# Local attention layers: the mask moved from TensorE to VectorE, the subtraction of the row maximum from VectorE to GpSimd, and the inverse norms computed by logarithm, exponential and a Newton step

## Chip, cores and metric

The kernel runs on one core of one Trainium2 chip. The time is the device time of one execution in microseconds. The kernel before has a median of 3261.2 us over three runs (3251.27, 3261.2 and 3266.76 us).

## What is computed

An input of 2048 tokens with 128 features goes through one global attention layer with 16 heads and a relation bias, and then through six local layers (`DEPTH` = 6). The change touches the local layers alone. Cut to that part, with 16 heads of 64 features and windows of 32 tokens, each local layer is:

```python
def l2norm(t):
    return t / jnp.maximum(jnp.linalg.norm(t, axis=-1, keepdims=True), 1e-12)

qkv = x @ Wqkv                                   # x is the shifted input
q = l2norm(q) * qs;  k = l2norm(k) * ksc
q = q * cos * scale + rotate_half(q) * sin * scale
k = k * cos * inv + rotate_half(k) * sin * inv
...
sim = jnp.einsum('bhwie,bhwje->bhwij', bq, bk2) * QK_SCALE      # 8.0
sim = jnp.where(mask, -jnp.finfo(sim.dtype).max, sim)
attn = jax.nn.softmax(sim, -1)
out = jnp.einsum('bhwij,bhwje->bhwie', attn, bv2)
x = out @ Wo + x
x = (a * gelu(gate)) @ W2 + b2 + x               # a, gate from layernorm(shift(x)) @ W1 + b1
```

The softmax runs over 64 keys: the window of the query and the one before it.

## The kernel before

The tokens are cut into `NB` = 16 blocks of 128. A local layer handles its blocks one after the other, so there are `NT` = 96 blocks in all. `local_layers` writes out one program per engine by hand, over the same list of `STEPS` (-1 to 101). In step `s` an engine works on several blocks at once, at different stages: projections for block `s`, transposes of q and k for `s-1`, scores, softmax and product with v for `s-2`, the output projection for `s-4`, the feed-forward part for `s-5` and `s-6`. Each engine executes its queue in the order of the program, and semaphores (`m[...]`) tie the engines together.

Names that matter below:

- TensorE in one step: scores S (L1255 mask, L1259), projection Q (L1235), transposes of k (L1242, from `kn`), projection K, output projection (L1284), transpose of `xn` (L1292), projection V, transposes of q, transpose of `xa` (L1308), W2 (L1314), transposes of the probabilities `pr`, transposes of `ot`, W1 (L1333), product with v (L1345).
- Its results lie in three PSUM buffers `R`, used in rotation in the order of `RING`. A use waits until the use three turns earlier has been read (`read_by`): Q waits for `g_done` of the feed-forward product in the step before, K waits for the reader of S, V waits for `sqq_done`.
- VectorE: maximum (L1513), subtraction (L1517), rotary products of q and k (L1504 to L1506), sums of squares (L1538, L1562), sum of the softmax (L1555), `bn_stats` (L1578), `ot` (L1589), `gT` (L1598), `xn` (L1607), in about this order.
- GpSimd: `kn` (L1446), root for q (L1435 maximum with 1e-24, L1437 power), scaling of `pr` by the inverse norms of q (L1455), the two rotary additions (L1460, L1462), `xmb` (L1468), `tab` (L1481), root for k (L1435, L1437), then `var` and `rstd` (L1489, L1493) of the layer norm.
- ScalarE: copies of kT (L1364, L1369), square of q (L1376), exponential (L1381), square of k (L1386), copy of v (L1391), copies of qT, prT and otT (L1352), Gelu (L1418), copies of xsT (L1425 to L1428). The table of the exponential and that of Gelu are loaded once each in a step.

The inverse norm of q isn't applied to q but to the scores: the kernel takes the maximum over unscaled scores, subtracts it, and multiplies the difference by the inverse norm. The mask is 0 or -1e25 and is written into PSUM as the first of two accumulated products.

Of the kernel before, what the change touches and what calls it, by code (L numbers as in the profile page):

```python
# [17 lines left out]
ALU = mybir.AluOpType  # L18
# [1039 lines left out]
def local_layers(nc, io):  # L1058
    with ExitStack() as ctx:
# [14 lines left out]
        mask = sb("mask", [P, 2, 2 * WIN], BF16)  # L1074
        ident = sb("ident2", [P, P])
        identb = sb("identb", [P, P], BF16)
# [9 lines left out]
        rnq = sb("rnq", [P, 2, LH])  # L1086
        rnk = sb("rnk", [P, LH])
# [33 lines left out]
            ssqq_done ssqk_done clampq_done clampk_done rnq_done rnk_done q_added k_added kn_done qT_done kT_done qT_ready  # L1121
            kT_ready s_done mx_done sub_done scaled_done exp_done sum_done rden_done pT_done pT_ready pv2_done o_ready
# [45 lines left out]
        with nc.Block() as block:  # L1168
            @block.sync
            def _(sp):  # L1170
                for dst, src in ((xm[:, 1:NB + 1, :], io["x1"].rearrange("(b p) d -> p b d", p=P)),
                                 (rope[:], io["rope"]), (mask32[:], io["mask"]), (ident[:], io["ident"])):
                    sp.dma_start(dst, src).then_inc(m["init_dma"], 16)
                load(sp, 0)

            @block.gpsimd
            def _(pool):
                n = 0
                for tile, value in ((half1[:], -0.5), (vs[:], 0.0), (v2[:], 0.0), (kT[:], 0.0), (zeros[:], 0.0), (xsT[:], 0.0)):
                    pool.memset(tile, value).then_inc(m["init_pool"], 1)  # L1180
                    n += 1

                pool.wait_ge(m["init_dve"], 2)
                pool.wait_ge(m["init_pool"], n)
                pool.tensor_scalar(mv16[:, :, 1], mv16[:, :, 1], 1e-5, None, ALU.add).then_inc(m["init_pool"], 1)
                pool.wait_ge(m["init_pool"], n + 1)
                pool.tensor_tensor(rs16[:], mv16[:, :, 1], half1[:, 0:NB], ALU.pow).then_inc(m["init_pool"], 1)

            @block.vector
            def _(dve):  # L1190
                dve.wait_ge(m["init_dma"], 16 * 4)
# [8 lines left out]
                dve.tensor_copy(identb[:], ident[:])  # L1200
                dve.tensor_copy(mask[:], mask32[:])
# [14 lines left out]
        read_by = {"S": "sub_done", "Q": "sqq_done", "kT": "kT_ready", "K": "sqk_done", "V": "v_ready", "qT": "qT_ready",  # L1216
# [6 lines left out]
        with nc.Block() as block:  # L1223
            @block.tensor
            def _(pe):
# [19 lines left out]
                for s in STEPS:  # L1245
                    n = s - 2
                    if has(n):
# [102 lines left out]
            def _(act):  # L1350
# [3 lines left out]
                for s in STEPS:  # L1354
# [52 lines left out]
                    if has(n):  # L1407
# [3 lines left out]
                        copy(otT[:].rearrange("p a b -> p (a b)"), flat[slot["oT", n]], "oT_ready")  # L1411
                    n = s - 5
# [18 lines left out]
            def _(pool):  # L1431
                def root(i, n, dst, summed, clamped, done):

                    pool.wait_ge(m[summed], n + 1)
                    pool.tensor_scalar(ssq[:, i, :], ssq[:, i, :], 1e-24, None, ALU.max).then_inc(m[clamped], 1)  # L1435
                    pool.wait_ge(m[clamped], n + 1)
                    pool.tensor_tensor(dst, ssq[:, i, :], half1[:], ALU.pow).then_inc(m[done], 1)  # L1437

                for s in STEPS:
                    n = s - 1  # L1440
                    if has(n):
                        pool.wait_ge(m["k_added"], n + 1)
                        pool.wait_ge(m["rnk_done"], n + 1)
                        if n > 0:
                            pool.wait_ge(m["kT_done"], n)
                        pool.tensor_tensor(kn[:].rearrange("p (h d) -> p h d", d=LD), k1[:].rearrange("p (h d) -> p h d", d=LD),  # L1446
                                           rnk[:].unsqueeze(2).broadcast_to([P, LH, LD]), ALU.mult).then_inc(m["kn_done"], 1)
                    if has(n):
                        root(0, n, rnq[:, n % 2, :], "ssqq_done", "clampq_done", "rnq_done")
                    n = s - 2  # L1450
                    if has(n):
                        pool.wait_ge(m["sub_done"], n + 1)
                        pool.wait_ge(m["rnq_done"], n + 1)
                        p = pr[:, n % 2].rearrange("p i a k -> p (i a) k")
                        pool.tensor_tensor(p, p, rnq[:, n % 2, :].unsqueeze(2).broadcast_to([P, LH, 2 * WIN]), ALU.mult)\  # L1455
                            .then_inc(m["scaled_done"], 1)
# [27 lines left out]
                    if has(n):  # L1484
                        root(1, n, rnk[:], "ssqk_done", "clampk_done", "rnk_done")
# [10 lines left out]
            def _(dve):  # L1496
# [11 lines left out]
                for s in STEPS:  # L1508
                    n = s - 2
                    if has(n):  # L1510
                        dve.wait_ge(m["s_done"], n + 1)
                        scores = flat[slot["S", n]].rearrange("p (h k) -> p h k", k=2 * WIN)
                        dve.tensor_reduce(mx[:], scores, AX.X, ALU.max).then_inc(m["mx_done"], 1)  # L1513
                        dve.wait_ge(m["mx_done"], n + 1)
                        if n > 1:
                            dve.wait_ge(m["pT_done"], n - 1)
                        dve.tensor_tensor(pr[:, n % 2].rearrange("p i a k -> p (i a) k"), scores,  # L1517
                                          mx[:].unsqueeze(2).broadcast_to([P, LH, 2 * WIN]), ALU.subtract)\
                           .then_inc(m["sub_done"], 1)
# [14 lines left out]
                    if has(n):  # L1534
                        dve.wait_ge(m["sqq_done"], n + 1)
                        if n > 0:
                            dve.wait_ge(m["rnq_done"], n)
# [20 lines left out]
                    if has(n):  # L1558
                        dve.wait_ge(m["sqk_done"], n + 1)
                        if n > 0:  # L1560
                            dve.wait_ge(m["rnk_done"], n)
# [169 lines left out]
```

## Time and profile before

| | |
|---|---|
| median of three runs | 3261.2 us |
| the profiled execution's own time | 3259.23 us |
| its span | 3257.4 us |
| global attention ends, first projection of the local layers | about 1500 us |
| TensorE busy | 2989.6 us (92%) |
| VectorE busy | 2433.3 us (75%) |
| GpSimd busy | 2283.7 us (70%) |
| ScalarE busy | 2033.3 us (62%) |

The span is the time between the first and the last instruction of the profile; 1.8 us of the execution lie around it. In the part after 1600 us GpSimd is busy for 375 of 400 us and TensorE for 394 of 400 us. A busy time of TensorE includes pipelining and isn't its best rate. In a timeline row the first number is the start in us from the span's start, the second the duration; "x4" says how many instructions were merged, and brackets show how long the engine was idle before it, and who released it. PEld is the loading of weights, which overlaps the products.

### The profile page before, as it was taken

How to read it: one execution, taken by the hardware profiler on the slowest of the kernel's cores; microseconds unless marked ns; L12 is line 12 of the kernel's file. 1: busy time of each engine (PE TensorE's matmuls, PEld its weight loads, DVE VectorE, ACT ScalarE, POOL GpSimd, SP SyncE). 2: the span in 40 equal slices, each digit the busy share in tenths (PEclk: the TensorE clock that was granted, in tenths of full speed). 3: DMA queues.
4: the chain of work that ended last, by engine and by line, in shares of the span. 5: the costliest groups of instructions: out<-in, count | busy, mean ns of one | idle time of the engine just before them, and what ended most of it. 6: DMA issues, size and time to landing. Idle time of an engine off the chain costs nothing.

```text
span 3257.4 us, 122555 instructions
## 1 busy us (share of the span) xinstructions
PE 2989.6 (92%) x53463; PEld 2278.3 (70%) x53463; DVE 2433.3 (75%) x3495; ACT 2033.3 (62%) x2669; POOL 2283.7 (70%) x1528
## 2 busy tenths in 40 slices
PE   4389999999999999994999999999999999999998
PEld 2267777777777777772677777777777777777776
DVE  4777777777777777734878778787877878787775
ACT  2345555555555555552677777777777777777775
POOL 1635555555555454306999999999999999999995
PEclk8589999999999999997999999999999999999999
DMA  5544445444444444404322233223223322322221
GB/s 116 101 80 86 77 84 88 85 79 86 81 83 84 78 84 84 84 5 124 82 64 63 69 79 83 59 68 96 66 67 81 83 58 69 94 68 67 68 76 45
DMA packets 253990, 251.90 MB, mean 77 GB/s; under 512 B 81999, under 2 KB 198624, under 8 KB 253328
## 3 DMA queue, kind: packets, MB, share of 16 engines
q1 hardware_dynamic: 251776, 243.67, 35.4%
q8 instruction: 423, 6.93, 1.0%
q14 instruction: 111, 0.91, 0.1%
q10 hardware_dynamic: 1680, 0.40, 0.1%
HBM read 96.22 MB, written 40.37 MB: 42 GB/s over the span
## 4 chain that ended last, share of the span: by engine, by line
PE 38%; ACT 8%; issue 4%; DVE 1%; POOL 1%; SPq 0%; DMA 0%; ACTq 0%; DVEq 0%; POOLq 0%
PE R L1235 11%; PE R L1242 10%; PE R L1345 5%; PE R L1259 5%; PE R L1333 4%; ACT kT L1364 3%; ACT sq L1376 3%; ACT kT L1369 2%; PE psB L1314 2%; PE R L1255 1%; PE psA L1308 0%; DVE mx L1513 0%; DVE ssq L1538 0%; DVE k L1504 0%; DMA xs_f<-xm 0%
## 5 line engine op out<-in xcount | busy, mean ns | idle before, releaser
L660 ACT ACTIVATE prob<-psS 128x1024 f32<-128x1024 f32 x512 | 524.0, 1024 | 598.7 <-PE psS L537 591.2
L824 DVE TENSOR_TENSOR colmax<-psS,colmax 128x1024 f32<-128x1024 f32 x480 | 587.3, 1224 | 309.1 <-PE psS L537 307.9
L537 PE MATMUL psS<-diag,pst 128*128 128x64 bf16 x16384 | 585.9, 195 | 26.6 <-issue 26.4
L1235 PE MATMUL R<-wqkv,xsT 128*128 128x512 f32 x1152 | 573.2, 620 | 37.1 <-ACT sq L1376 31.3
L537 PEld LDWEIGHTS psS<-diag,pst 128*128 128x128 f16 x16384 | 519.1, 99 | 87.3 <-issue 33.9
L529 PE MATMUL psS<-qst,kst 48*128 48x128 bf16 (+1 forms) x8192 | 382.0, 221 | 125.6 <-DMA pst<-p_parts 89.9
L758 POOL TENSOR_TENSOR rel<-rel,rec 128x1024 f32<-128x1024 f32 x64 | 151.7, 2370 | 484.7 <-DVE rec L837 484.7
L1364 ACT ACTIVATE kT<-R 64x1024 f32<-64x1024 f32 x192 | 195.7, 1019 | 423.7 <-PE R L1242 422.6
L529 PEld LDWEIGHTS psS<-qst,kst 48*128 48x128 bf16 (+1 forms) x8192 | 236.1, 95 | 282.4 <-issue 173.0
L1235 PEld LDWEIGHTS R<-wqkv,xsT 128*128 128x128 f32 x1152 | 196.9, 190 | 227.4 <-issue 159.6
L571 PE MATMUL psO<-prob,v 128*9 128x128 f32 x8192 | 326.6, 275 | 12.6 <-issue 11.3
L1437 POOL TENSOR_TENSOR rnq<-ssq,half 128x16 f32<-128x16 f32 x96 | 281.7, 2934 | 8.0
L1437 POOL TENSOR_TENSOR rnk<-ssq,half 128x16 f32<-128x16 f32 x96 | 281.2, 2930 | 8.0
L1589 DVE TENSOR_TENSOR ot<-R,rden 128x1024 f32<-128x1024 f32 x96 | 117.6, 1225 | 208.8 <-PE R L1345 208.7
L837 DVE RECIPROCAL rec<-tot 128x128 f32<-128x128 f32 x256 | 238.7, 939 | 0.0
L1460 POOL TENSOR_TENSOR q<-q 128x1024 f32<-128x1024 f32 x96 | 227.0, 2364 | 6.8 <-DVE q L1506 6.8
L1462 POOL TENSOR_TENSOR k<-k 128x1024 f32<-128x1024 f32 x96 | 227.8, 2372 | 0.3 <-DVE k L1506 0.3
L1284 PEld LDWEIGHTS psA<-wo,otT 128*128 128x128 f32 x1536 | 186.3, 192 | 44.4 <-issue 44.4
L571 PEld LDWEIGHTS psO<-prob,v 128*9 128x9 f32 x8192 | 174.0, 90 | 43.7 <-issue 15.1
L1259 PEld LDWEIGHTS R<-kT,qT 128*32 128x32 f32 x6144 | 162.0, 110 | 40.8 <-issue 40.7
L1345 PE MATMUL R<-v,prT 128*32 128x128 f32 x6144 | 187.6, 274 | 2.8 <-ACT prT L1352 2.8
L1259 PE MATMUL R<-kT,qT 128*32 128x128 f32 x6144 | 187.8, 274 | 0.0
(190 smaller groups left out, 6076.2 us busy)
## 6 DMA issues: line engine op xcount, KB each, us to landing
v<-vs SPq DMA_DIRECT2D x576, 128.0 KB, 2.4
pst<-p_parts SPq DMA_DIRECT2D x512, 128.0 KB, 4.9
p_parts<-stage SPq DMA_DIRECT2D x64, 512.0 KB, 3.0
v<-vs SPq DMA_DIRECT2D x384, 64.0 KB, 2.0
wqkv<-in_L_ffn_Wqkv SPq DMA_DIRECT2D x18, 512.0 KB
q_stack<-qpart SPq DMA_DIRECT2D x6, 512.0 KB
qst<-q_stack SPq DMA_DIRECT2D x32, 96.0 KB, 5.4
wo<-in_L_ffn_Wo SPq DMA_DIRECT2D x6, 512.0 KB
```

Source lines behind the costliest of these rows:

```text
L529: pe.matmul(dst[:, hp, P * p:P * (p + 1)], kst[r, pair, P * jb:P * (jb + 1)], qst[r, par, pair, :], start=(p == 0), stop=False, skip_group ...
L537: last = pe.matmul(o, pst[:, par, g, P * jb:P * (jb + 1)], diag[:, par, g, h0:h0 + HH // 2, :], start=False, stop=(g == NG - 1), skip_grou ...
L571: last = pe.matmul(psO[32 * c:32 * c + HD + 1, P * s:P * (s + 1)], v9[:, jb, HH * half + hl, :], prob[:, jb % 2, col:col + P], start=(jb = ...
L660: act.activation(prob[:, st % 2, :], psS[:, slot_of("b", st)].rearrange("p a b -> p (a b)"), ACT.Exp)\
L824: dve.tensor_tensor(dst, src, dst, ALU.max).then_inc(a_read, 1)
L837: dve.reciprocal(rec[:, r, cols], tot[:, r, cols]).then_inc(rr_done, 1)
L1235: last = pe.matmul(R[slot[kind, n]][:, c, :], xsT[:, n % 3, :], w[:, INNER * which + 512 * c:INNER * which + 512 * (c + 1)], start=True, s ...
L1242: last = pe.transpose(o[:, P * i:P * (i + 1)], src[:, P * i:P * (i + 1)], ident[:])
L1259: last = pe.matmul(o[WIN * w:WIN * (w + 1), P * i:P * (i + 1)], qT[:, par, i, WIN * w:WIN * (w + 1)], kT[:, par, i, :, WIN * w:WIN * (w + 2)],
L1345: last = pe.matmul(o[WIN * w:WIN * (w + 1), P * i:P * (i + 1)], prT[:, i, WIN * w:WIN * (w + 1)], v2[:, par, w, :, i, :], start=True, stop ...
L1364: act.activation(kT[r, par, :, hp, WIN:WIN + P], keys[r], ACT.Copy)
L1437: pool.tensor_tensor(dst, ssq[:, i, :], half1[:], ALU.pow).then_inc(m[done], 1)
```

## The change

- TensorE no longer multiplies the mask in. The scores start their own PSUM groups.
- VectorE adds the mask from `mask32` while it moves the scores from PSUM into `pr` (new semaphore `masked_done`), and then takes the maximum from `pr`. The PSUM buffer of S is free after the addition.
- GpSimd subtracts the maximum from `pr` in place, after `mx_done`, and then scales `pr` as before.
- The two powers on GpSimd (L1437) go. One maximum with 1e-24 over both sums of squares (128x32) stands in their place; ScalarE takes the logarithm and the exponential of -0.5 times it (128x32 each), placed after the copy of otT and ahead of Gelu; GpSimd then makes a Newton step of four instructions on 128x32. Everything that waited for `rnq_done` or `rnk_done` waits for `rn_done`. The power for `rstd` (L1493) stays.
- ScalarE loads the set `natural_log_exp_and_others` by an instruction of its own ahead of the softmax's exponential, behind the wait for `scaled_done`.
- Two small copies at the start of the local layers go.

```diff
-                        mk = mask[:, 0 if n % NB == 0 else 1, :]
-                        for half in range(2):
-                            pe.matmul(R[slot["S", n]][:, half, :], identb[:], mk.unsqueeze(1).broadcast_to([P, PAIRS, 2 * WIN]),
-                                      start=True, stop=False, skip_group_check=True)
                         for i in range(PAIRS):
                             for w in range(NW):
                                 last = pe.matmul(o[WIN * w:WIN * (w + 1), P * i:P * (i + 1)], qT[:, par, i, WIN * w:WIN * (w + 1)],
                                                  kT[:, par, i, :, WIN * w:WIN * (w + 2)],
-                                                 start=False, stop=True, skip_group_check=True)
+                                                 start=True, stop=True, skip_group_check=True)
...
                         act.wait_ge(m["scaled_done"], n + 1)
+                        act.preload_act_table_set("natural_log_exp_and_others")
...
+                    n = s
+                    if has(n):
+                        act.wait_ge(m["clamp_done"], n + 1)
+                        act.activation(logs[:], ssq[:].rearrange("p a h -> p (a h)"), ACT.Ln).then_inc(m["log_done"], 1)
+                        act.wait_ge(m["log_done"], n + 1)
+                        if n > 1:
+                            act.wait_ge(m["scaled_done"], n - 1)
+                        act.activation(rn[:, n % 2].rearrange("p a h -> p (a h)"), logs[:], ACT.Exp, scale=-0.5)\
+                           .then_inc(m["root_done"], 1)
...
-                    if has(n):
-                        root(0, n, rnq[:, n % 2, :], "ssqq_done", "clampq_done", "rnq_done")
                     n = s - 2
                     if has(n):
+                        pool.wait_ge(m["mx_done"], n + 1)
+                        p = pr[:, n % 2].rearrange("p i a k -> p (i a) k")
+                        pool.tensor_tensor(p, p, mx[:].unsqueeze(2).broadcast_to([P, LH, 2 * WIN]), ALU.subtract)\
+                            .then_inc(m["sub_done"], 1)
                         pool.wait_ge(m["sub_done"], n + 1)
-                        pool.wait_ge(m["rnq_done"], n + 1)
...
-                        root(1, n, rnk[:], "ssqk_done", "clampk_done", "rnk_done")
+                        x, y, t = ssq[:].rearrange("p a h -> p (a h)"), rn[:, n % 2].rearrange("p a h -> p (a h)"), newton[:]
+                        pool.wait_ge(m["ssqk_done"], n + 1)
+                        pool.tensor_scalar(x, x, 1e-24, None, ALU.max).then_inc(m["clamp_done"], 1)
+                        pool.wait_ge(m["root_done"], n + 1)
+                        pool.tensor_tensor(t, y, y, ALU.mult).then_inc(m["newton_done"], 1)
+                        pool.wait_ge(m["newton_done"], 3 * n + 1)
+                        pool.tensor_tensor(t, t, x, ALU.mult).then_inc(m["newton_done"], 1)
+                        pool.wait_ge(m["newton_done"], 3 * n + 2)
+                        pool.tensor_scalar(t, t, -0.5, 1.5, ALU.mult, ALU.add).then_inc(m["newton_done"], 1)
+                        pool.wait_ge(m["newton_done"], 3 * n + 3)
+                        pool.tensor_tensor(y, y, t, ALU.mult).then_inc(m["rn_done"], 1)
...
-                        dve.tensor_reduce(mx[:], scores, AX.X, ALU.max).then_inc(m["mx_done"], 1)
-                        dve.wait_ge(m["mx_done"], n + 1)
                         if n > 1:
                             dve.wait_ge(m["pT_done"], n - 1)
-                        dve.tensor_tensor(pr[:, n % 2].rearrange("p i a k -> p (i a) k"), scores,
-                                          mx[:].unsqueeze(2).broadcast_to([P, LH, 2 * WIN]), ALU.subtract)\
-                           .then_inc(m["sub_done"], 1)
+                        p = pr[:, n % 2].rearrange("p i a k -> p (i a) k")
+                        allowed = mask32[:, 0 if n % NB == 0 else 1, :].unsqueeze(1).broadcast_to([P, LH, 2 * WIN])
+                        dve.tensor_tensor(p, scores, allowed, ALU.add).then_inc(m["masked_done"], 1)
+                        dve.wait_ge(m["masked_done"], n + 1)
+                        if n > 0:
+                            dve.wait_ge(m["sub_done"], n)
+                        dve.tensor_reduce(mx[:], p, AX.X, ALU.max).then_inc(m["mx_done"], 1)
```

## Rows read from the trace of the kernel before

**Rows 1.** Waits, 1600 to 3200 us: total, times, longest.
```profile
PE R L1235 <- ACT sq L1376: 24.3, 87, 0.3
```
**Rows 2.** Chain that ended last: start, us, what; the mask's products.
```profile
2828.31 0.54 PE R L1255 x2
```
**Rows 3.** Timeline of one step of the ring, all engines: start, duration.
```profile
2812.97 1.22 DVE L1513 TENSOR_REDUCE mx<-R 128x16 f32<-128x1024 f32 x1 [0.16 <-PE R L1259]
...
2814.23 1.22 DVE L1517 TENSOR_TENSOR pr<-R,mx 128x1024 f32<-128x1024 f32 x1
...
2816.06 1.90 POOL L1455 TENSOR_TENSOR pr<-pr,rnq 128x1024 f32<-128x1024 f32 x1
...
2817.92 2.37 POOL L1460 TENSOR_TENSOR q<-q 128x1024 f32<-128x1024 f32 x1
...
2821.05 0.14 PEld L1242 LDWEIGHTS R<-ident,q 128*128 128x128 f32 x1 [0.24 <-issue]
...
2822.36 0.27 PE L1308 MATMUL psA<-ident,xa 128*128 128x128 f32 x1
...
2823.15 1.21 DVE L1562 TENSOR_REDUCE ssq<-sq 128x16 f32<-128x1024 f32 x1
...
2824.01 1.04 PE L1242 MATMUL R<-ident,ot 128*128 128x128 f32 x8
...
2824.44 0.25 POOL L1435 TENSOR_SCALAR ssq<-ssq 128x16 f32<-128x16 f32 x1 [0.73 <-DVE ssq L1562]
...
2825.50 1.05 ACT L1352 ACTIVATE otT<-R 128x1024 f32<-128x1024 f32 x1
...
2828.38 1.22 DVE L1589 TENSOR_TENSOR ot<-R,rden 128x1024 f32<-128x1024 f32 x1 [2.07 <-PE R L1345]
...
2829.52 0.85 DVE L1598 SCALAR_TENSOR_TENSOR gT<-R,b_cols,gl 128x128 f32<-128x128 f32 x3
...
2830.30 0.34 DVE L1607 TENSOR_SCALAR xn<-xs_f,mv,rstd 128x128 f32<-128x128 f32 x1
...
2830.66 0.30 PEld L1235 LDWEIGHTS R<-wqkv,xsT 128*128 128x128 f32 x2 [0.20 <-issue]
...
2830.80 1.23 DVE L1513 TENSOR_REDUCE mx<-R 128x16 f32<-128x1024 f32 x1 [0.16 <-PE R L1259]
```
**Rows 4.** Groups by line, 1600 to 3257 us: busy, mean ns; idle before.
```profile
L1468 POOL TENSOR_TENSOR xmb<-xm,b_rows 128x128 f32<-128x128 f32 x96 | 44.4, 463 | 2.3 <-DVE xa L1574 2.3
...
L1428 ACT ACTIVATE xsT<-psA 64x1 f32<-64x1 f32 x83 | 12.8, 154 | 0.0
```
**Rows 5.** Timeline of an early step, in which TensorE waits for GpSimd.
```profile
1518.32 1.90 POOL L1446 TENSOR_TENSOR kn<-k,rnk 128x1024 f32<-128x1024 f32 x1
...
1520.27 0.86 PEld L1242 LDWEIGHTS R<-ident,kn 128*128 128x128 f32 x8 [3.05 <-POOL kn L1446]
...
1521.20 1.88 PE L1235 MATMUL R<-wqkv,xsT 128*128 128x512 f32 x4
```
**Rows 6.** Timelines of GpSimd, then VectorE, in a step with late `kn`.
```profile
2240.06 0.23 POOL L1489 TENSOR_SCALAR var<-mv 128x1 f32<-128x1 f32 x1 [0.85 <-DVE mv L1582]
...
2240.92 1.90 POOL L1446 TENSOR_TENSOR kn<-k,rnk 128x1024 f32<-128x1024 f32 x1
```
```profile
2241.81 1.09 DVE L1607 TENSOR_SCALAR xn<-xs_f,mv,rstd 128x128 f32<-128x128 f32 x1
2242.83 1.21 DVE L1513 TENSOR_REDUCE mx<-R 128x16 f32<-128x1024 f32 x1
```
**Rows 7.** Line 1607 in all steps: duration in ns, minimum/median/maximum.
```profile
L1607 DVE TENSOR_SCALAR xn<-xs_f,mv,rstd x96: 333/346/1658, 1581.2 to 3247.0; 128x128 f32<-128x128 f32 x96
```
**Rows 8.** Timeline of the drain, after the last projections.
```profile
3208.40 1.90 POOL L1455 TENSOR_TENSOR pr<-pr,rnq 128x1024 f32<-128x1024 f32 x1
...
3209.22 1.28 ACT L1381 ACT_TABLE_LOAD   x1
```

More of the change, by code:

```diff
@@ L1073, in local_layers @@
         mask32 = sb("mask32", [P, 2, 2 * WIN])
-        mask = sb("mask", [P, 2, 2 * WIN], BF16)
         ident = sb("ident2", [P, P])
-        identb = sb("identb", [P, P], BF16)
         xsT = sb("xsT", [P, 3, P])
@@ L1085, in local_layers @@
         ssq = sb("ssq", [P, 2, LH])
-        rnq = sb("rnq", [P, 2, LH])
-        rnk = sb("rnk", [P, LH])
+        rn = sb("rn", [P, 2, 2, LH])
+        newton = sb("newton", [P, 2 * LH])
+        logs = sb("logs", [P, 2 * LH])
         kn = sb("kn", [P, INNER])
@@ L1120, in local_layers @@
         names = """init_dma init_dve init_pool w_dma xT_done xT_ready q_done k_done v_done sqq_done sqk_done tq_done tk_done
-            ssqq_done ssqk_done clampq_done clampk_done rnq_done rnk_done q_added k_added kn_done qT_done kT_done qT_ready
-            kT_ready s_done mx_done sub_done scaled_done exp_done sum_done rden_done pT_done pT_ready pv2_done o_ready
+            ssqq_done ssqk_done clamp_done log_done root_done newton_done rn_done q_added k_added kn_done qT_done kT_done qT_ready
+            kT_ready s_done masked_done mx_done sub_done scaled_done exp_done sum_done rden_done pT_done pT_ready pv2_done o_ready
             oT_done oT_ready wo_done x2_done st_done lnv_done eps_done rstd_done xn_done xnT_done xnT_ready h_done
@@ L1199, in _ @@
                 dve.memset(xm[:, 0, :], 0.0)
-                dve.tensor_copy(identb[:], ident[:])
-                dve.tensor_copy(mask[:], mask32[:])
                 dve.wait_ge(m["init_pool"], 8)
@@ L1215, in local_layers @@
         earlier = {t: turns[i - 3] for i, t in enumerate(turns) if i >= 3}
-        read_by = {"S": "sub_done", "Q": "sqq_done", "kT": "kT_ready", "K": "sqk_done", "V": "v_ready", "qT": "qT_ready",
+        read_by = {"S": "masked_done", "Q": "sqq_done", "kT": "kT_ready", "K": "sqk_done", "V": "v_ready", "qT": "qT_ready",
                    "pT": "pT_ready", "oT": "oT_ready", "h": "g_done", "O": "o_ready"}
@@ L1431, in _ @@
             def _(pool):
[L1432 to L1437, printed above, removed]
                 for s in STEPS:
@@ L1442, in _ @@
                         pool.wait_ge(m["k_added"], n + 1)
-                        pool.wait_ge(m["rnk_done"], n + 1)
+                        pool.wait_ge(m["rn_done"], n + 1)
                         if n > 0:
@@ L1446, in _ @@
                         pool.tensor_tensor(kn[:].rearrange("p (h d) -> p h d", d=LD), k1[:].rearrange("p (h d) -> p h d", d=LD),
[L1447 to L1449 removed]
+                                           rn[:, n % 2, 1, :].unsqueeze(2).broadcast_to([P, LH, LD]), ALU.mult).then_inc(m["kn_done"], 1)
                     n = s - 2
                     if has(n):
+                        pool.wait_ge(m["mx_done"], n + 1)
+                        p = pr[:, n % 2].rearrange("p i a k -> p (i a) k")
+                        pool.tensor_tensor(p, p, mx[:].unsqueeze(2).broadcast_to([P, LH, 2 * WIN]), ALU.subtract)\
+                            .then_inc(m["sub_done"], 1)
                         pool.wait_ge(m["sub_done"], n + 1)
[L1453 to L1455 removed]
+                        pool.wait_ge(m["rn_done"], n + 1)
+                        pool.tensor_tensor(p, p, rn[:, n % 2, 0, :].unsqueeze(2).broadcast_to([P, LH, 2 * WIN]), ALU.mult)\
                             .then_inc(m["scaled_done"], 1)
@@ L1536, in _ @@
                         if n > 0:
-                            dve.wait_ge(m["rnq_done"], n)
+                            dve.wait_ge(m["rn_done"], n)
                         dve.tensor_reduce(ssq[:, 0, :], sq[:].rearrange("p (h d) -> p h d", d=LD), AX.X, ALU.add)\
@@ L1560, in _ @@
                         if n > 0:
-                            dve.wait_ge(m["rnk_done"], n)
+                            dve.wait_ge(m["rn_done"], n)
                         dve.tensor_reduce(ssq[:, 1, :], sq[:].rearrange("p (h d) -> p h d", d=LD), AX.X, ALU.add)\
```

## The prediction

> **What bounds the kernel now.** I read the groups by line first. They show GpSimd with two powers of 2.93 us in each step, which looks like the engine to relieve. The waits say otherwise: in the local layers TensorE waits for ScalarE's square of q, 87 times for 0.3 us at most [rows 1], and for next to nothing else. The chain that ended last is accordingly almost all TensorE, with one passage through ScalarE's copies of kT and the square, and the mask's products lie on it with 0.54 us a step [rows 2]. The timeline of one step then gives the order on each engine. From one start of the maximum on VectorE to the next it takes 2830.80 - 2812.97 = 17.83 us [rows 3]. Below, all times are us after that start (0), before the change:
>
> maximum 0, subtraction 1.26, GpSimd's scaling 3.09, its q addition 4.95, TensorE's first load of weights for the q transposes 8.08, transpose of xa 9.39, end of the ot transposes 12.08, ScalarE's copy otT 12.53, VectorE's ot 15.41, gT 16.55, xn 17.33, load for projection Q 17.69, maximum again 17.83 [rows 3].
>
> Two things are to be seen there. First, the q addition ends at 7.32, and TensorE wants it at 8.08: GpSimd has only 0.76 us in hand. Second, VectorE runs ot, gT and xn back to back after the product with v, and is done at 17.67, 0.16 us before it starts the maximum. Projection Q waits, by the ring of PSUM buffers, for gT, which ends at 17.40, and Q's load is at 17.69. So the stretch after the product with v is nearly as long on VectorE (ot, gT, xn) as on TensorE (mask, scores).
>
> **Part by part.**
>
> *The mask's products.* 0.54 us a step leave TensorE, 96 times, 52 us if nothing else were late [rows 2]. But VectorE is late next. From ot to the next maximum it needs 1.14 + 0.78 + 0.27 = 2.19 us (xn lasts 0.34 and the next instruction starts 0.07 before its end) against the 2.42 us it has now. Without the mask, the scores would be done 0.54 earlier and VectorE 0.23 earlier. So this edit is worth 0.23 us a step at the most, 22 us in all.
>
> *Addition and maximum on VectorE.* The addition has the form of the subtraction it replaces, one operand in PSUM, 1.22 us. The maximum now reads SBUF; the sum of squares from SBUF takes 1.21 [rows 3]. Sum unchanged: 1.26 from the first start to the second, then 1.22. The maximum is done at 2.48, as the subtraction was. K's buffer is free 1.26 earlier, which is worth nothing while V waits for ScalarE.
>
> *The subtraction on GpSimd.* It has the form of the scaling (in place, 128x1024, one operand broadcast): 1.90 [rows 3]. A release of GpSimd by VectorE takes 0.08 (sum of squares ends at 2824.36, GpSimd starts at 2824.44 [rows 3]); I take 0.08 too for a wait on GpSimd's own result. So: subtraction 2.56 to 4.46, scaling 4.54 to 6.44, q addition 6.40 to 8.76 (it starts 0.04 before the scaling's end, as now [rows 3]). TensorE is released by GpSimd 0.05 later (kn ends at 1520.22, load at 1520.27, and the next group's product starts 0.93 after that load [rows 5]). So the load is at 8.81 and the transpose of xa at 9.74, against 9.39 now: **everything behind it on TensorE is 0.35 us late**, with the power for q gone from that place already. Then ot starts at 15.41 + 0.35 = 15.76, gT 16.90, xn 17.68, next addition 17.95. That alone is a period of 17.95, 0.12 more than now: the mask's gain is spent.
>
> *The roots.* GpSimd loses two powers and one of two small maxima, 5.86 + 0.25 us a step, and gains four instructions on 128x32. The total work of GpSimd falls, but what counts is where kn ends, because of VectorE's xn. In rows 6 kn runs from 2240.92 to 2242.82 and xn, normally 0.35, lasts 1.09 and ends at 2242.90, 0.08 after kn; the next instruction of VectorE starts at 2242.83. The longest xn has 1.66 us [rows 7], and it too ended 0.09 after its kn. So xn stands until kn is through. The Trainium skill ("SBUF — State Buffer", section "SBUF: two separate sides") has the rule: a VectorE instruction in a two-port mode and a GpSimd instruction exclude each other for their whole length; the trace agrees by these rows.
>
> So I follow kn. The ot transposes end at 12.08 + 0.35 = 12.43, and the copy otT starts at about 12.5, as now, and ends at 13.55. GpSimd's small maximum is long done by then (q and k additions, xmb and tab end at about 12.2). The logarithm starts at 13.5. ScalarE's price for 128x32 isn't in the trace: 64x1 takes 0.154 [rows 4], a 128x1024 copy 1.05 [rows 3]; I take 0.2, near the small row, and 0.07 for each release. Exponential done at 13.95, GpSimd starts at 14.02. The Newton instructions lie between 0.25 (128x16, one operand [rows 3]) and 0.463 (128x128, two operands [rows 4]); I take 0.26, since 32 columns are near 16, and 0.08 behind each: 4 x 0.34 = 1.36, var starts at 15.38. From var to kn 0.86 and kn 1.90 [rows 6]: kn runs from 16.24 to **18.14**. xn can't end before 18.22, and the addition starts at 18.15. That is later than 17.95, so it sets the period: 18.15, or 0.32 a step more than now. Projection Q, released by gT's end at 17.75, isn't held by this, nor are the k transposes behind it, which come at about 19.2.
>
> Bounds: with Newton at 0.25 and ScalarE at 0.15 the period is 18.0; below 17.95 it can't come, by VectorE's own sequence. With Newton at 0.463 and ScalarE at 0.35 it is 19.25, but the small rows are far nearer.
>
> *ScalarE.* Logarithm and exponential (0.45) lie ahead of Gelu's table load and Gelu: Gelu ends at about 16.2, needed at 16.90. Cover 0.7. The softmax's exponential: its table load used to run ahead of the wait (in the drain it starts at 3209.22, while the scaling ends at 3210.30 [rows 8]); now it stands behind it. In the steady ring the square ends at about 6.4 and the scaling at 6.44, so nothing is lost. In the last two steps there are no projections to hide anything: the chain from the scores to the exponential gets 1.90 + 0.08 for the subtraction and up to 1.28 for the load, less 0.6 where the power for q used to hold the scaling, and less 0.54 for the mask: together about +5 us. In the first two steps, ahead of the first explicit load, logarithm and exponential may need a load each, ahead of the copy xsT that releases the next projection: +2 to 3 us.
>
> **Sum.** Full ring from step 5 to 95: 91 steps x 0.32 = 29; drain 5; start 2. 3259.2 + 36 = 3295 us. The profiled execution is 2 us below the median of the runs, 3261.2, which is within their spread.
>
> **Rivals.**
> *A: kn isn't what holds the addition* (small instructions at the low end, or xn slips in before kn). Then VectorE's sequence gives 17.95 to 18.0: 91 x 0.12 to 0.17 + 7 = 18 to 22, so 3277 to 3281. If start and drain cost nothing: 3270. Chance 0.28, half of it within 0.5%.
> *B: the path through GpSimd has more cover than I see*, and q's addition holds nobody. Then VectorE sets the period after the mask's removal, 17.83 - 0.23 = 17.60: 91 x -0.23 + 7 = -14, 3245 us. For it: GpSimd is idle for over 4 us a step. Against: its addition ends at 8.76 where TensorE now loads at 8.08. It decides from a q addition done by 8.4. Chance 0.09.
> *C: the small instructions are dear* (period 18.6 to 19.2): 3335 to 3390. Chance 0.13.
> *D: the explicit table set isn't kept* and the logarithm or the exponential behind it brings a load of 1.28 each [rows 8]. kn would be 1.3 or 2.6 later: 91 x 1.6 = +150, 3410 us or more. The Trainium skill ("ScalarE: Activation LUTs", section "Table sets: the hidden batching unit") says this set holds both functions, against that rival. Chance 0.05.
> Main forecast: 0.45. The range 3268 to 3340 takes in the main case with its bounds, A, and the near end of C.
>
> Against 3261.2, 0.5% is 16 us, about what a measurement of this kernel can tell from no change. Slower by more: 0.45 + 0.13 + 0.05 + half of A = 0.77, less 0.04 for a main case that comes out small: 0.73. The same: the other half of A, these 0.04 and 0.01 of B: 0.19. Faster: 0.08.
>
> **What would show it.** A period of 18.1 to 18.2 between two additions of the mask; xn longer than 0.35 in every step and ending 0.08 after kn; TensorE waiting for "POOL q" ahead of the q transposes, 0.7 to 0.9 us a step in its loads; projection Q waiting for gT, not for TensorE; no more wait for "ACT sq"; subtraction at 1.90, Newton at 0.26 each; two table loads a step. The prediction is wrong if xn stays at 0.35, if Newton costs above 0.4, or if TensorE's wait is still on ScalarE.

## The result and the profile after

The changed kernel takes 3269.27 us (median of 18 runs, 3263.93 to 3281.44), the kernel before beside it 3251.19 us (18 runs, 3243.22 to 3266.76). The ratio is 1.0059, with a 95% interval of 1.0046 to 1.0072: slower by 18 us. The forecast was 3295, with 36 us of loss. The sign was right and the size twice too large; whether the loss is above the 0.5% that the prediction takes as its line isn't settled, since the interval begins at 1.0046.

The profiled execution of the changed kernel took 3264.24 us (span 3262.4), only 5 us more than that of the kernel before. The two can't be compared as wholes: the first projection of the local layers begins 15.35 us earlier in it (the transpose of `xa` at 1485.89 against 1501.24), in a stage that wasn't changed. So here and below times are read from that transpose on ("local layers"), and split at the starts of VectorE's first instruction on the scores of block 4 and of block 94:

| us | before | after | difference | forecast |
|---|---|---|---|---|
| first transpose of `xa` to block 4 | 98.84 | 104.98 | +6.1 | +2 |
| block 4 to block 94 | 1605.23 | 1610.99 | +5.8 | +29 |
| block 94 to the end | 52.09 | 60.54 | +8.45 | +5 |
| local layers | 1756.16 | 1776.51 | +20.35 | +36 |
| usual period | 17.83 | 17.88 | +0.05 | +0.32 |

The local layers' difference fits the 18 us of the medians. Over two thirds of the loss lie outside the steady ring.

One step of the ring in the changed kernel, the rows that answer to [rows 3] (timeline: start, duration, engine, line):

```profile
2826.45 1.21 DVE L1524 TENSOR_TENSOR pr<-R,mask 128x1024 f32<-128x1024 f32 x1
...
2827.69 1.22 DVE L1528 TENSOR_REDUCE mx<-pr 128x16 f32<-128x1024 f32 x1
...
2828.99 1.90 POOL L1448 TENSOR_TENSOR pr<-pr,mx 128x1024 f32<-128x1024 f32 x1 [2.55 <-DVE mx L1528]
...
2830.97 1.90 POOL L1452 TENSOR_TENSOR pr<-pr,rn 128x1024 f32<-128x1024 f32 x1
...
2832.84 2.37 POOL L1457 TENSOR_TENSOR q<-q 128x1024 f32<-128x1024 f32 x1
...
2832.90 1.28 ACT L1373 ACT_TABLE_LOAD   x1 [0.23 <-POOL pr L1452]
...
2834.12 0.14 PEld L1239 LDWEIGHTS R<-ident,q 128*128 128x128 f32 x1 [0.24 <-issue]
2834.19 1.06 ACT L1375 ACTIVATE pr<-pr 128x1024 f32<-128x1024 f32 x1
...
2839.67 0.27 ACT L1409 ACTIVATE logs<-ssq 128x32 f32<-128x32 f32 x1
...
2840.28 0.24 POOL L1486 TENSOR_TENSOR newton<-rn 128x32 f32<-128x32 f32 x1 [1.26 <-ACT rn L1413]
...
2842.43 1.90 POOL L1442 TENSOR_TENSOR kn<-k,rn 128x1024 f32<-128x1024 f32 x1
...
2842.81 0.85 DVE L1607 SCALAR_TENSOR_TENSOR gT<-R,b_cols,gl 128x128 f32<-128x128 f32 x3
...
2843.58 0.83 DVE L1616 TENSOR_SCALAR xn<-xs_f,mv,rstd 128x128 f32<-128x128 f32 x1
2843.78 0.30 PEld L1232 LDWEIGHTS R<-wqkv,xsT 128*128 128x128 f32 x2 [0.70 <-issue]
...
2844.34 1.21 DVE L1524 TENSOR_TENSOR pr<-R,mask 128x1024 f32<-128x1024 f32 x1
```

From one addition of the mask to the next: 17.89. The addition, L1524, starts 0.01 after `kn` has ended at 2844.33, and `xn` has grown from 0.34 to 0.83 and ends 0.08 after `kn`, as forecast. Two rows speak against the forecast. TensorE loads the q transposes at 2834.12, while GpSimd's q addition runs until 2835.21: it doesn't wait for that addition. And ScalarE's table load starts at 2832.90, right behind the scaling, with ScalarE idle for 0.23 before it.

The chain that ended last, same step (start, us, what):

```profile
2824.57 1.87 POOL kn L1442
2826.44 2.51 issue
...
2828.99 1.91 POOL pr L1448
...
2830.97 1.91 POOL pr L1452
...
2832.90 1.28 ACT L1373
...
2834.19 0.55 ACT pr L1375
...
2839.67 0.28 ACT logs L1409
...
2841.89 0.57 POOL rstd L1500
2842.46 1.87 POOL kn L1442
```

This view is the one to learn from. TensorE, which carried [rows 2], is gone from it. The chain runs over subtraction, scaling, table load, exponential, then ScalarE's queue without a gap (square of k, v, qT, prT, otT) to the logarithm, and back to `kn`. Between the end of `kn` and the subtraction stands "issue" for 2.51 us: there the view has no releaser, because what ties VectorE to `kn` isn't a semaphore. In the timeline that hole is the end of `xn`, the addition and the maximum.

The waits, 1600 to 3200 us (total, times, longest), for [rows 1]:

```profile
POOL pr L1448 <- DVE mx L1528: 226.8, 89, 2.6
...
PE R L1232 <- DVE gT L1607: 40.6, 89, 1.1
PE R L1232 <- ACT sq L1369: 31.8, 89, 0.4
...
ACT L1373 <- POOL pr L1452: 21.3, 89, 0.5
```

TensorE now waits both for gT (0.46 us a step) and for the square (0.36). The prediction had named a wait that is still on ScalarE as a sign against itself. GpSimd waits 2.55 us a step for the maximum, and it is busy for 603 of 800 us (2000 to 2800 us) against 748 before: the work taken from it became idle time.

The price of the small instructions: logarithm 0.26, exponential 0.23, Newton 0.24, 0.25, 0.22 and 0.25, subtraction 1.90.

### The profile page after: what moved, and what is told of

Read it like the earlier page. It is cut to its first block, busy times and chain, and to the rows that moved or that the text cites. A ratio compares the mean times of both kernels' runs of the same rounds, so it can differ in the third digit from the quotient of the medians.

```text
span 3262.4 us, 122750 instructions
## 1 busy us (share of the span) xinstructions
PE 2942.5 (90%) x53271; PEld 2272.3 (70%) x53271; DVE 2482.3 (76%) x3493; ACT 2077.2 (64%) x2869; POOL 1977.9 (61%) x1720
## 4 chain that ended last, share of the span: by engine, by line
POOL 21%; ACT 16%; issue 15%; PE 1%; POOLq 0%; ACTq 0%; DVE 0%
POOL pr L1448 5%; POOL pr L1452 5%; POOL kn L1442 5%; ACT L1373 4%; ACT prT L1345 3%; ACT vs L1385 3%; POOL rstd L1500 2%; ACT pr L1375 2%; ACT sq L1380 1%; ACT qT L1345 1%; ACT logs L1409 1%; POOL newton L1488 1%; ACT otT L1345 1%; POOL rn L1492 1%; POOL newton L1486 1%
## 5 line engine op out<-in xcount | busy, mean ns | idle before, releaser
L1357 ACT ACTIVATE kT<-R 64x1024 f32<-64x1024 f32 x192 | 195.4, 1018 | 369.4 <-PE R L1239 368.3
L1448 POOL TENSOR_TENSOR pr<-pr,mx 128x1024 f32<-128x1024 f32 x96 | 182.6, 1903 | 247.2 <-DVE mx L1528 247.2
L1277 PE MATMUL psA<-wo,otT 128*128 128x128 f32 x1536 | 187.3, 275 | 0.0
L1452 POOL TENSOR_TENSOR pr<-pr,rn 128x1024 f32<-128x1024 f32 x96 | 182.7, 1903 | 7.5
```

Of the source, the lines that this page charges most:

```text
L1277: last = pe.matmul(psA[:, 0:D], otT[:, i, :], wo[:, n // NB % 2, D * i:D * (i + 1)], start=(i == 0), stop=(i == PAIRS - 1))
L1448: pool.tensor_tensor(p, p, mx[:].unsqueeze(2).broadcast_to([P, LH, 2 * WIN]), ALU.subtract)\
L1452: pool.tensor_tensor(p, p, rn[:, n % 2, 0, :].unsqueeze(2).broadcast_to([P, LH, 2 * WIN]), ALU.mult)\
```

## The experiments

Each run was compared with runs of the kernel before on the same chip. From one chip to the next that kernel's median lies between 3246.4 and 3262.0 us, so the ratios compare between runs and the times only roughly. The period, the usual time from one step to the next, is read from each run's trace. Two theories stood at the start. Theory 1: the step is set by the chain of the view above, closed by `xn` standing until `kn` is through. Theory 2: the prediction's own, or the loop through projection Q and gT; each expectation says which.

**The table load ahead of the wait.**

```diff
-                        act.wait_ge(m["scaled_done"], n + 1)
                         act.preload_act_table_set("natural_log_exp_and_others")
+                        act.wait_ge(m["scaled_done"], n + 1)
```

> The changed kernel, with the load of the table set ahead of ScalarE's wait for the scaling and not behind it. Theory 1 (the step is set by the chain maximum, subtraction, scaling, table load, exponential, ScalarE's queue up to the logarithm, Newton, kn, and xn, which stands until kn is through): the load starts when the square of q ends, 0.23 us earlier, the exponential too, and everything up to kn; the period falls from 17.88 to about 17.65 us, and the drain by 2 x 1.28 us: about 3246 us against 3269. Theory 2 (kn's place is set by TensorE's transposes of ot, and the exponential has cover, as the prediction said): the period stays at 17.88, and only the drain gains, 3266 us.

Measured: ratio to before 1.0005 (0.9992 to 1.0017), 3250.0 us, period 17.66, local layers 1756.7. From its timeline:

```profile
2712.94 1.91 POOL L1452 TENSOR_TENSOR pr<-pr,rn 128x1024 f32<-128x1024 f32 x1
...
2714.64 1.28 ACT L1372 ACT_TABLE_LOAD   x1
...
2715.93 1.06 ACT L1375 ACTIVATE pr<-pr 128x1024 f32<-128x1024 f32 x1
```

The load starts 0.2 us before the scaling ends and not behind it. 0.22 us a step and 4.4 us in the drain (from block 94 on it takes 56.2 for 60.5) are together worth the whole loss; the start stays as slow as it was. Theory 1 holds: the exponential had no cover.

**xn behind the maximum of the next step.** VectorE's `xn` (L1616 to L1617 with its waits) goes behind L1528, with `n = s - 5` for `n = s - 4`.

> The changed kernel, with VectorE's xn moved behind the maximum of the next step, so that the addition of the mask follows gT directly. Theory 1 (the addition starts late because xn stands until kn is through): xn lasts 0.35 us again, the addition starts 0.5 us earlier after gT, the scaling is done before the square of q, and the period falls to the loop Q, transposes of k, copies of kT, square, V, product with v, ot, gT, Q, which is 6.82 + 8.72 + 1.14 + 0.85 + 0.12 = 17.65 us: about 3249 us. Theory 2 (xn's length isn't what holds the step; the loop through Q and gT is by itself 17.88): no change, 3269 us.

Measured: 0.9993 (0.9979 to 1.0006), 3243.9 us, period 17.66, local layers 1756.6.

```profile
2710.29 1.90 POOL L1442 TENSOR_TENSOR kn<-k,rn 128x1024 f32<-128x1024 f32 x1
...
2711.43 1.21 DVE L1524 TENSOR_TENSOR pr<-R,mask 128x1024 f32<-128x1024 f32 x1
...
2712.68 1.22 DVE L1528 TENSOR_REDUCE mx<-pr 128x16 f32<-128x1024 f32 x1
...
2713.81 0.34 DVE L1535 TENSOR_SCALAR xn<-xs_f,mv,rstd 128x128 f32<-128x128 f32 x1
```

The addition starts 0.76 us before `kn` ends, and `xn` takes 0.34 again. The subtraction is held a little in its turn (1.93 for 1.90). Both edits end at the same 17.66, as the loop through Q and gT asks.

**xn from PSUM.**

```diff
+                dve.memset(psB[:, D:2 * D], 0.0)
...
-                        dve.tensor_scalar(xn[:], xs_f[:, n % 2, :], mv[:, 0:1], rstd[:, 0:1], ALU.subtract, ALU.mult)\
+                        dve.tensor_scalar(xn[:], psB[:, D:2 * D], mv[:, 0:1], rstd[:, 0:1], ALU.subtract, ALU.mult)\
```

> The changed kernel, with xn at its old place but reading zeros from PSUM in place of the normalised rows; the layer norm's input is left out, so the feed-forward part computes with something else. Theory 1 (xn stands because an instruction of VectorE between SBUF and SBUF and one of GpSimd exclude each other): with its input in PSUM it takes 0.40 us, as xnT does, no longer ends with kn, the addition of the mask starts 0.4 us earlier, and the period is that of the loop through Q and gT, 17.66 us: about 3249 us. Theory 2 (xn stands for another reason, a wait or GpSimd's traffic in SBUF as such): xn stays at 0.83 and the period at 17.88, 3269 us.

Measured: 0.9992 (0.9981 to 1.0003), 3243.9 us, period 17.66. The line in all steps, duration in ns as minimum/median/maximum:

```profile
L1617 DVE TENSOR_SCALAR xn<-psB,mv,rstd x96: 393/397/411, 1568.9 to 3228.6; 128x128 f32<-128x128 f32 x96
```

With its input in PSUM `xn` never takes more than 0.411, at the same place beside the same `kn`; in the changed kernel the median is 0.829, the maximum 1.916. So it is the operand in SBUF that makes it stand. This is the rule of the Trainium skill ("SBUF — State Buffer", section "SBUF: two separate sides"), and this run agrees. In the traces the two don't exclude each other quite to the end, though. In the kernel before, `kn` is still running for 0.25 us when `xn` starts at 2830.30 [rows 3], and `xn` takes its 0.34 all the same:

```profile
2828.65 1.90 POOL L1446 TENSOR_TENSOR kn<-k,rnk 128x1024 f32<-128x1024 f32 x1
```

**The two halves of the change, each alone on the kernel before.**

> The kernel before, with the roots by logarithm, exponential and Newton step alone; mask on TensorE and subtraction on VectorE as before. Theory 1: kn ends about 0.3 us after VectorE wants xn, so the maximum starts 0.3 us later against projection Q, but the scaling is still done long before the square of q ends, so nothing feeds back: period 17.83 to 17.95. The first two steps still cost some 5 us by their extra table loads. 3256 to 3268 us. Rival (the roots' edit is the whole loss): 3269 us with a period of 17.88 and a longer drain.

Measured: 1.0041 (1.0023 to 1.0058), 3261.7 us; period 17.83; local layers +14.6 us, of it 6.5 until block 4 and 5.4 behind block 94. `xn` takes 0.82 and moves the maximum later, but the loop through TensorE doesn't feel it. The roots cost nothing in the usual step here, 2.7 us in all between block 4 and block 94, and some 12 us at the ends.

> The kernel before, with the mask's addition on VectorE and the subtraction on GpSimd alone; both powers stay on GpSimd. GpSimd waits 0.73 us of each step in the kernel before; with 1.98 us more it has none left, and the period is its own queue: 17.83 - 0.73 + 1.98 = 19.08 us. 94 steps x 1.25 = 117 us, so about 3370 us. If the subtraction ran beside idle time that isn't seen, it would be less, down to a period of 17.65 and 3240 us.

Measured: 1.0385 (1.0370 to 1.0401), 3372.5 us, period 19.06, as expected. From its timeline:

```profile
2717.37 1.90 POOL L1442 TENSOR_TENSOR kn<-k,rnk 128x1024 f32<-128x1024 f32 x1
2717.44 1.92 DVE L1608 TENSOR_SCALAR xn<-xs_f,mv,rstd 128x128 f32<-128x128 f32 x1 [0.37 <-POOL rstd L1492]
```

`xn` lasts as long as `kn`, 1.92. GpSimd's own queue is the period. So neither half helps by itself: the mask's half has no room on GpSimd while the powers are there, and the roots' half brings nothing while TensorE's loop is the limit.

**Both mends together, the load first in the step.** As the run with `xn` behind the maximum, and

```diff
                 for s in STEPS:
+                    if s < NT + 2:
+                        act.preload_act_table_set("natural_log_exp_and_others")
...
                         act.wait_ge(m["scaled_done"], n + 1)
-                        act.preload_act_table_set("natural_log_exp_and_others")
```

> The changed kernel with xn behind the maximum of the next step, and the table set loaded as ScalarE's first instruction of every step, also in the first steps. The loop through Q and gT stays, so the period stays at 17.66 us, as each of the two edits gave alone. In the first two steps the four extra loads of 1.28 us go, some 4 to 5 us, and in the drain the load no longer stands behind the scaling, 2.5 us: about 3249 - 7 = 3242 us, 0.2% faster than the kernel before. If the loads are a limit of the step after all, the period falls below 17.6.

Measured: 0.9940 (0.9926 to 0.9954), 3226.5 us, period 17.60, local layers 1739.6: faster than either kernel. The stretch up to block 4 is 98.9 us, 6.1 less than in the changed kernel; 2.2 of them had come with `xn` (102.8 in that run), so the loads make 3.9, for 4 to 5 expected. The period is 0.06 better than expected; no run says why.

**gT ahead of ot.** As the run before, with VectorE's gT ahead of ot.

> As the run before, and gT ahead of ot on VectorE, so that projection Q, whose PSUM buffer waits for gT, is released 0.6 to 0.7 us earlier. Theory 1 (the loop Q, kT copies, square, V, product with v, ot, gT sets the 17.66 us): the period falls, by 0.2 to 0.35 us, until the late addition of the mask (behind ot, now about 1.0 us after Q) feeds back through scaling and exponential: 17.3 to 17.45 us, 3210 to 3225 us. Rival: the late addition feeds back at once, and the period stays at 17.6 or rises: 3240 us or more.

Measured: 0.9995 (0.9982 to 1.0008), 3245.6 us, period 17.78. The rival was right:

```profile
2829.53 0.87 ACT L1422 ACTIVATE gl<-R,b_cols 128x128 f32<-128x128 f32 x3
...
2830.43 0.86 DVE L1607 SCALAR_TENSOR_TENSOR gT<-R,b_cols,gl 128x128 f32<-128x128 f32 x3 [2.50 <-ACT gl L1422]
...
2831.22 1.21 DVE L1616 TENSOR_TENSOR ot<-R,rden 128x1024 f32<-128x1024 f32 x1
...
2832.35 1.21 DVE L1525 TENSOR_TENSOR pr<-R,mask 128x1024 f32<-128x1024 f32 x1
```

gT now waits for Gelu, ot and the addition come behind it, and the addition is 0.94 after projection Q (load at 2831.41) where it was 0.19 before it. Scaling and exponential are late again. Projection Q comes 3.79 us after the product with v where it came 4.16 after it, 0.37 earlier and not 0.6 to 0.7, and that is lost at once.

**The square of q ahead of the small copies of kT.** ScalarE squares q between the two large copies of kT (L1357) and the two small ones (L1362), so that V is released earlier. Three kernels have this edit.

> The changed kernel with the move of the square alone. Theory 1 (the changed kernel's 17.88 us is the chain maximum, subtraction, scaling, load, exponential, ScalarE's queue to the logarithm, Newton, kn, xn): the square's place in ScalarE's queue doesn't change when the exponential starts, so the period stays at 17.88 us, 3269 us. Theory 2 (the loop through Q, square, V and gT is 17.88 by itself): the period falls by some 0.6 us, to 3215 us.

Measured on the changed kernel: 1.0115 (1.0096 to 1.0134), 3297.6 us beside 3262.0, period 18.08. Not the gain of theory 2, but not the 17.88 of theory 1 either.

```profile
2814.05 1.21 DVE L1526 TENSOR_TENSOR pr<-R,mask 128x1024 f32<-128x1024 f32 x1
...
2818.87 1.02 ACT L1363 ACTIVATE sq<-R 128x1024 f32<-128x1024 f32 x1 [0.43 <-DVE q L1515]
...
2820.57 1.28 ACT L1375 ACT_TABLE_LOAD   x1
...
2827.48 0.26 ACT L1411 ACTIVATE logs<-ssq 128x32 f32<-128x32 f32 x1
```

The square waits here for VectorE's product with q, so the load starts 6.52 after the addition (6.45 in the changed kernel), and the logarithm 13.43 after it (13.22). These 0.21 are the 0.20 of the period: what feeds the chain costs in full, as theory 1 says, and I hadn't counted that the edit would feed it. Of the 0.21, 0.07 lie ahead of the load; most of the rest (0.11) arises between the exponential and the square of k, for which the rows name no cause.

> The kernel before with that move of the square alone. TensorE waits there 0.28 us a step for the square and for nothing else, so only this can go: period 17.83 - 0.28 = 17.55 us, about 25 us less than the kernel before: 3222 us. It is the share of the move that doesn't need the mask off TensorE.

Measured on the kernel before: 1.0005 (0.9991 to 1.0019), period 17.85. The expectation failed. V no longer waits for the square, but the transposes of `pr` wait 0.25 us a step for the square of k. So the kernel before stood on two things that were late by nearly the same: the square of q, and ScalarE's queue from the table load on. The view of waits [rows 1] showed the first of them. That the load's place is what holds the queue is only argued here; the next run tests it.

> The kernel before, with the square of q ahead of the small copies of kT and the table set loaded as ScalarE's first instruction in every step; mask on TensorE, powers on GpSimd. The run with the moved square alone stayed at 17.85 us, because ScalarE's queue from the table load on held the transposes of the probabilities. Without the load in that place TensorE is left with its own queue: 17.83 - 0.28 = 17.55 us, about 25 us less than the kernel before. If so, the changed kernel with the same two edits (17.03 us) owes 0.5 us a step to the mask having left TensorE. If it too comes to 17.1 us, the change has no part in it.

Measured on the kernel before with the load first in the step as well: 0.9880 (0.9862 to 0.9897), 3213.3 us beside 3252.5, period 17.30, better than the 17.55 expected. Its row for 2000 to 2800 us (us, then busy time and count of PE, PEld, DVE, ACT, POOL; clock; share of DMA, GB/s):

```profile
2000.00:2800.00 800.00, 799.34 (x9709) 614.06 (x9710) 655.55 (x1017) 618.84 (x879) 771.14 (x555) 1.00 0.31 77
```

TensorE is busy for 799.34 of 800 us. The wait for the square was worth more than the 0.28 that its bracket shows. From the transpose of `xn` to the start of projection V it takes 0.11 us here and 0.54 in the kernel before, and from there to the transposes of q 1.72 for 1.82: together 0.53, which is 17.83 - 17.30.

> The changed kernel with xn behind the maximum, the table set loaded first in every step, and ScalarE's square of q moved between the two large and the two small copies of kT (ahead of 0.77 us of copies). Theory (the loop Q, kT transposes, kT copies, square, V, product with v, ot, gT, Q sets the 17.60 us): V is released up to 0.8 us earlier, of which TensorE's own queue leaves about 0.6, and nothing else is late yet: period about 17.0 us, 91 x 0.6 = 55 us less than 3226, so about 3172 us. If ScalarE's total queue or VectorE's rotary products are next, the period stays above 17.3 us, 3200 us.

Measured on the changed kernel with all three edits (`xn`, load, square): 0.9793 (0.9770 to 0.9815), 3191.3 us beside 3262.0, period 17.03. The same row:

```profile
2000.00:2800.00 800.00, 777.31 (x9763) 619.06 (x9762) 659.54 (x1034) 643.52 (x986) 635.50 (x659) 1.00 0.32 78
```

This is the fastest version. With the same two edits on ScalarE, the kernel before reaches 17.30, and with the change (and `xn` moved) it is 17.03. So the change is worth 0.27 us a step, not the 0.5 that was expected, and only where ScalarE no longer stands in the way. It isn't the 0.54 that TensorE was relieved of: TensorE has 22.69 us idle in 800 again, its waits being for gT. As the two kernels also differ in where `xn` stands, the 0.27 holds for the change with that move; what the move alone would do for the kernel before wasn't run.

## Why the prediction was right or wrong

*The mask's products.* Right in kind: they left 0.54, and VectorE's ot and gT took most of it back. From the product with v to projection Q it takes 4.16 us for 4.31, so 0.15 are left, for 0.23 forecast. The runs that were freed of the chain stopped at 17.60 to 17.66, where the prediction had 17.60 for that case (its rival B).

*Addition, maximum, subtraction, scaling.* Right to 0.05: subtraction at 2.54 after the addition and 1.90 long, scaling at 4.52.

*The q addition releases the q transposes, TensorE is 0.35 late.* This step was wrong, and no size was: TensorE's transposes in step `s` are of block `s - 1` (`n = s - 1` ahead of the wait for `q_added`), GpSimd's addition in step `s` is of block `s`. The addition that TensorE waits for was done a step ago. The row was there before the change: the addition's place beside the load says nothing of a dependency, and I took two instructions that lie close in time for a pair. With it falls "GpSimd has only 0.76 us in hand", and so does the bound that the period "can't come" below 17.95: it came to 17.88. Without the 0.35 the prediction's own terms put `kn` at 15.89 and the period at 17.80: 91 x -0.03 + 7 = 4 us of loss in place of 36.

*xn stands until kn is through.* Right, and shown by three runs: with `xn` moved, with its input in PSUM, and in the mask's half alone, where it lasts 1.92. It is the closing piece of the step in the changed kernel.

*The place of kn.* Forecast 16.24 after the addition, measured 15.98 (2842.43 - 2826.45). The reason was wrong twice. Nothing was late on TensorE by the q addition, which puts the logarithm at 13.15 and not at 13.5; but ScalarE's queue, and with it the copy otT and the logarithm, hung on the exponential, and the logarithm came at 13.22. So this second error put back only 0.07 of the 0.35. The small instructions were priced right: Newton with its waits 1.30 from the first start to that of `var` for 1.36, logarithm and exponential with their waits 0.61 for 0.52.

*ScalarE's table load costs nothing in the steady ring.* Wrong. I set the end of the square (6.4) beside the end of the scaling (6.44), called that covered, and didn't follow what hangs on it. The square ended at 6.22 and the scaling at 6.42, so the load waits for the scaling in each step, 0.23 us at the median and 0.15 at the least, and everything behind it in ScalarE's queue is on the chain. The run with the load ahead of the wait gives 17.66 for 17.88.

*Start and drain.* Mis-sized: 7 forecast, 14.6 measured. Two things are mixed in them: the instructions that were added, and TensorE's clock, which the prediction left out. In the first two steps there are two loads each, ahead of the copy that releases the next projection:

```profile
1499.44 1.28 ACT L1409 ACT_TABLE_LOAD   x1
...
1500.98 1.28 ACT L1413 ACT_TABLE_LOAD   x1
1502.27 0.23 ACT L1413 ACTIVATE rn<-logs 128x32 f32<-128x32 f32 x1
1502.41 0.25 ACT L1428 ACTIVATE xsT<-psA 64x128 f32<-64x128 f32 x1
```

L1409 and L1413 load for the logarithm and again for the exponential, and only then does the copy xsT run. That is 2.57 us in each of two steps. Taking both mends together gives 6.1 us back, 3.9 with the loads and 2.2 with the place of `xn`. But that isn't a full account of how the start became 6.1 us longer than before. In the changed kernel projection V of two early blocks ran at a lower clock:

```profile
1527.56 3.56 PE L1232 MATMUL R<-wqkv,xsT 128*128 128x512 f32 x4 [2.25 <-ACT sq L1369]
```

The granted clock was 0.53 there, near the lower level of 1.2 GHz, and the same happened at 1544.55 (3.60); in the kernel before projection V took 1.98 in these steps. That is 3.2 us. The run with both mends has the two slow projections too (3.63 and 3.64), so how much of the 6.1 is the clock's stays open. In the drain the subtraction and the load behind the scaling stand in the open:

```profile
3206.39 1.90 POOL L1452 TENSOR_TENSOR pr<-pr,rn 128x1024 f32<-128x1024 f32 x1
...
3208.31 1.28 ACT L1373 ACT_TABLE_LOAD   x1 [2.37 <-POOL pr L1452]
...
3210.72 1.97 PE L1239 MATMUL R<-ident,pr 128*128 128x128 f32 x8 [4.22 <-ACT pr L1375]
```

The load begins 0.02 after the scaling ends, where in [rows 8] it was long running, and TensorE has waited 4.22 us when the transposes of `pr` start (1.88 before). From VectorE's first instruction on the scores to these transposes it takes 2.5 us more than before for block 94 and 3.2 for block 95, 5.8 in all. This is the term that the prediction had at "about +5" (its own summands give 2 x 2.12 = 4.2), and it was nearly right.

What it left out comes behind: the transposes run at 1.97 us for 1.09. From their start to W1, first the changed kernel, then the kernel before (stretch, its length, busy time and count of PE, PEld, DVE, ACT, POOL; clock; share of DMA, GB/s):

```profile
3210.72:3213.88 3.16, 3.16 (x17) 3.16 (x18) 1.97 (x5) 2.01 (x2) 0.77 (x2) 0.55 0.07 20
```
```profile
3211.63:3213.43 1.80, 1.80 (x17) 1.80 (x17) 1.59 (x3) 1.67 (x2) 0.00 (x0) 1.00 0.11 25
```

TensorE is busy all the time in both. The granted clock is 0.55 after 4.22 us of idleness, near the lower level (1.2 GHz), and 1.00 (2.4 GHz) after 1.88 us. That costs 1.36 us, and for block 95, up to the product with v, another 1.10 (5.96 us at 0.52 for 4.86 at 0.65). So 2.5 of the drain's 8.45 us are the clock's, and no sum of instruction times at full clock contains them. That the longer waits bring the lower clock is likely but not shown: in the kernel before, the transposes of block 95 took 1.97 us too, after only 1.55 us of idleness.

*The sum.* 91 x 0.32 = 29 was the term that failed; it measured 5.8 (0.05 a step and some single late steps). The ends made 14.6 for 7. That the sign came out right is owed to the ends and, in the ring, to luck: without the wrong pair the forecast has the ring a little faster (17.80), and the 0.05 of loss came from ScalarE's queue, which it had called covered. Rival A (period 17.95, 3277 to 3281) came nearest, though by another mechanism than its own. Rival B (chance 0.09) had the true premise, that the q addition holds nobody, but not the chain through `kn`, and its 17.60 is where the mended kernels stand. Rival D didn't happen: behind the first explicit load there are two loads a step, for the softmax and for Gelu.

## What to carry to other kernels

Before two instructions are called a pair, compare the block index in both loops: in a staggered ring, neighbours in time often belong to different blocks, and one wrong pair, at 0.35 us a step, made all of the ring's 29 us in this forecast. Where an engine's queue has no gaps, a late instruction early in it is late for everything behind it, whatever cover its own result has; follow the queue to the next wait of another engine. And a change that relieves an engine is to be read against the second loop, not the first: here the kernel before had two limits at 17.83 and 17.85 us and the changed kernel had two at 17.88 and 17.6 to 17.66, and the change paid only after two instructions of ScalarE and one of VectorE had been moved. Where a change lengthens the waits of TensorE at the ends of a ring, read the granted clock there as well as the waits.

## What the runs showed of the hardware

- An instruction of VectorE between SBUF and SBUF (128x128, with two scalars from SBUF) took 0.33 to 0.35 us alone, and up to 1.92 us beside one of GpSimd; wherever it was lengthened, it ended 0.07 to 0.09 us after it. From PSUM it took 0.39 to 0.41. The other way round the cost is small: GpSimd's subtraction took 1.94 at the median when `xn` came just before it, and 1.90 otherwise.
- No view of waits shows this. It appears as a longer instruction (0.83 for 0.34), and as "issue" in the chain (2.51 us).
- A table load takes 1.28 us and the exponential starts 0.01 after it (2834.18, 2834.19). The Trainium skill ("ScalarE: Activation LUTs", section "What ACT_TABLE_LOAD costs") adds some 1.4 us for a drain; no load in these traces shows it.
- A load that the compiler placed went ahead of the wait: in the drain of the kernel before it started at 3209.22, and the scaling ended at 3210.30 [rows 8]. One written behind the wait kept that place (0.02 us after the scaling) and cost 0.22 us a step here.
- After 4.22 us of idleness TensorE's granted clock was 0.55 and its eight transposes took 1.97 us; after 1.88 us it was 1.00, and they took 1.09. But in the kernel before they took 1.97 for block 95 after 1.55 us, so the length of the last pause doesn't decide alone.
